# h is transposed one unit later in the last seven units of a gated cross-attention and mixture-of-experts kernel

## The reference

```python
def layernorm(x): return (x - mean(x)) / sqrt(var(x) + 1e-5)
# stage 1: attention over ctx, rotary embedding on q and k, masked softmax
q, k, v = layernorm(x) @ Wq, ctx @ Wk, ctx @ Wv
attn = softmax(mask(rope(q) @ rope(k).T / sqrt(128)))
x = x + tanh(g_xattn) * ((attn @ v) @ Wo)
# stage 2: router and experts on h = layernorm(x)
h = layernorm(x)
ratio = mean|h[text rows]| / (mean|h[vision rows]| + 1e-8)
scores = softmax([h, ratio] @ gate_w + gate_b)
top_val, top_idx = top_k(scores, 2)          # normalised; experts chosen by row 0 of the batch
expert_e(h) = act_e(h @ w1[e] + b1[e]) @ w2[e] + b2[e]   # act: tanh, gelu, silu
x = x + tanh(g_ffn) * sum_i top_val[i] * expert_(top_idx[i])(h)
```

## Time and profile before

| | us |
|---|---|
| median of 3 runs | 736.51 |
| the runs | 736.07, 736.51, 739.14 |
| profiled execution | 737.81 |
| its span | 736.0 |
| PE busy in the span | 704.6 (96%) |
| VectorE, ScalarE, GpSimd busy | 558.4, 357.0, 402.6 |
| drain of 7 units, from the first Y projection | from 574.12 |

### The profile page before, as it was taken

The page is one execution under the profiler, slowest core; times in us unless marked ns, Lnnn a source line. Parts: engine busy times, 40 slices in busy tenths (PEclk is TensorE's granted clock), DMA queues, the critical chain, the costliest instruction groups (busy, mean ns, idle before and its releaser), DMA issues.

```text
span 736.0 us, 11337 instructions
## 1 busy us (share of the span) xinstructions
PE 704.6 (96%) x3478; PEld 587.7 (80%) x3478; DVE 558.4 (76%) x924; ACT 357.0 (49%) x955; POOL 402.6 (55%) x340
## 2 busy tenths in 40 slices
PE   5798899899999999999999999999999879999998
PEld 3686688688888888888888888888888766788886
DVE  4977778778878787878888887878787984378832
ACT  5522452455554545454545545454545574872130
POOL 5653524665766666666657566666666541383020
PEclk9999999999999999999999999999999999999999
DMA  8695465432133131212213112222222310240101
GB/s 285 223 288 204 171 216 185 129 101 64 52 87 87 58 87 57 82 61 72 71 36 109 58 56 86 86 57 87 58 77 67 104 69 29 58 115 14 58 1 58
DMA packets 66111, 71.10 MB, mean 97 GB/s; under 512 B 8592, under 2 KB 42384, under 8 KB 66064
## 3 DMA queue, kind: packets, MB, share of 16 engines
q1 hardware_dynamic: 65680, 69.51, 30.1%
q0 software_dynamic: 384, 1.05, 0.4%
HBM read 51.66 MB, written 18.87 MB: 96 GB/s over the span
## 4 chain that ended last, share of the span: by engine, by line
PE 82%; DVE 6%; issue 5%; ACT 3%; POOL 3%; DMA 1%; SPq 0%; POOLq 0%; ACTq 0%; DVEq 0%
PE q L263 34%; PE y L253 28%; PE o L590 5%; PE s L542 5%; PE pt L464 4%; PE s L544 2%; PE o L253 1%; PE pt L253 1%; ACT prob L840 1%; POOL roped L1033 1%; DVE rot L1141 1%; DVE rot L1142 1%; DVE rot L1140 1%; DMA wraw<-in_L_xattn_Wk 1%; POOL scores L1033 1%
## 5 line engine op out<-in xcount | busy, mean ns | idle before, releaser
L263 PE MATMUL q<-xT_hi,big 128*128 128x512 f32 x704 | 235.9, 400 | 0.4 <-issue 0.4
L253 PE MATMUL y<-big,split 128*128 128x512 f32 (+1 forms) x784 | 193.0, 392 | 2.9 <-DVE split L1113 2.9
L253 PEld LDWEIGHTS y<-big,split 128*128 128x128 f32 x784 | 147.9, 189 | 34.5 <-DVE split L1113 3.9
L263 PEld LDWEIGHTS q<-xT_hi,big 128*128 128x128 f32 x704 | 132.2, 188 | 27.3 <-issue 0.6
L263 PE MATMUL q<-xT_lo,big 128*128 128x512 f32 x352 | 136.9, 389 | 0.0
L1060 POOL TENSOR_TENSOR roped<-rot 128x512 f32<-128x512 f32 x59 | 76.4, 1295 | 104.1 <-DVE rot L1142 104.1
L840 ACT ACTIVATE prob<-scores,nmax 128x128 f32<-128x128 f32 x256 | 99.8, 391 | 22.2 <-DVE nmax L1245 22.2
L828 ACT ACTIVATE big<-roped 128x512 fp32r<-128x512 f32 x64 | 40.5, 633 | 142.3 <-POOL roped L1060 137.6
L1076 POOL TENSOR_TENSOR prob<-prob,prec 128x512 f32<-128x512 f32 x64 | 66.6, 1040 | 50.7 <-DVE prec L1259 50.7
L1064 POOL TENSOR_TENSOR big<-roped,big 128x512 fp32r<-128x512 f32 x64 | 82.8, 1294 | 13.4 <-ACT big L828 13.4
L1052 POOL TENSOR_TENSOR big<-wraw,big 128x512 fp32r<-128x512 f32 x64 | 83.2, 1300 | 1.9 <-ACT big L820 1.9
(11 more groups left out here) (170 smaller groups left out, 1141.9 us busy)
## 6 DMA issues: line engine op xcount, KB each, us to landing
k_scratch<-split SPq DMA_DIRECT2D x16, 512.0 KB, 3.5
v_scratch<-split SPq DMA_DIRECT2D x16, 512.0 KB, 3.6
wraw<-in_L_xattn_Wq SPq DMA_DIRECT2D x32, 256.0 KB
wraw<-in_L_xattn_Wo SPq DMA_DIRECT2D x32, 256.0 KB
kv<-k_scratch SPq DMA_DIRECT2D x64, 128.0 KB, 2.5
kv<-v_scratch SPq DMA_DIRECT2D x64, 128.0 KB, 2.8
wraw<-in_L_ffn_w SPq DMA_DIRECT2D x28, 256.0 KB
rows<-ctx_t SPq DMA_DIRECT2D x8, 256.0 KB
```

The source lines that it names most:

```text
L253: mm = pe.matmul(bank_[:, :], stationary(s, c), moving(m, c), start=(c == 0 and n == 0), stop=(c == EC - 1 and n == 2))
L263: mm = pe.matmul(bank_[:, :].rearrange("p (b t) -> p b t", b=BH), weights[s][:, c, h * P:(h + 1) * P], source[m][:, half * BH:(half + 1) * ...
```

## The change

In the drain, PE transposes h of batch b - 2 instead of b - 1 in unit b, so that two more transposes lie behind it; `first_layer(0)` and `gate_products(0)` follow the Y projection of b = 6, and `first_layer(1)` the drain. ScalarE does the expert chunk after the exponentials, and the row and the h copy (now of batch b - 3) ahead of them. VectorE does `h_neg_mean` ahead of the scores, the h split (b - 3) ahead of the reciprocal, and `h_stats` at the end of the unit. GpSimd splits the expert chunk one unit later and does `h_pow` after the probabilities. No instruction is added or taken away.

```diff
--- before.py
+++ after.py
@@ -565,8 +565,7 @@
                 if past in VALUES_IN:
                     value_tile(2 * B - len(VALUES_IN) + VALUES_IN.index(past))
                 if drain and b == LAG_Y - 1:
-                    gate_products(0)
-                    first_layer(1)
+                    h_transpose(b - 2)
                 if not drain and past == LAG_Y:
                     pe.wait_ge(u_lo, 4 * B - 1)
                 if has(LAG_Y):
@@ -590,10 +589,11 @@
                         mm = pe.matmul(obank[:, :], kv[:, bs % NKV, 2 + s, :], split[:, 1, m, :],
                                        start=(n == 0), stop=(n == 2))
                     mm.then_inc(o_done, 1)
-                if drain and b >= 1:
-                    h_transpose(b - 1)
-                if drain and b == LAG_Y - 2:
+                if drain and 2 <= b < LAG_Y - 1:
+                    h_transpose(b - 2)
+                if drain and b == LAG_Y - 1:
                     first_layer(0)
+                    gate_products(0)
 
             def h_transpose(hb):
                 pe.wait_ge(h_row, hb + 1)
@@ -679,6 +679,8 @@
                 pe.matmul(sbank[:, 128:128 + B * NX], sel[:, 2, :], score.rearrange("p b e -> p (b e)"),
                           start=True, stop=True).then_inc(tok0_mm, 1)
 
+            h_transpose(B - 3)
+            first_layer(1)
             h_transpose(B - 2)
             first_layer(2)
             h_transpose(B - 1)
@@ -818,8 +820,6 @@
                     buf = wb[par] if b < EC else wa[1 - par]
                     act.wait_ge(w_in[b % NW], (g * 2 + ((W_A + b) // NW + 1)) * 16)
                     act.activation(buf[0][:, b % EC, :], wraw[:, b % NW, :], ACT.Copy).then_inc(w_hi, 1)
-                else:
-                    w_expert_hi(W_A + KVH * W_PER + b)
                 if has(1):
                     _, bq = lagged(par, b, 1)
                     act.wait_ge(q_roped, i)
@@ -831,6 +831,10 @@
                     if past >= LAG_P + 1:
                         act.wait_ge(o_done, i - LAG_P)
                     act.activation(split[:, 1, 0, :], pbank[:, :], ACT.Copy).then_inc(p_hi, 1)
+                if drain and b >= 1:
+                    norm_row(1, b - 1)
+                if drain and b >= 3:
+                    h_hi_(b - 3)
                 if has(LAG_S):
                     act.wait_ge(s_max, i - LAG_S + 1)
                     if past >= LAG_S + 1:
@@ -841,16 +845,13 @@
                                            bias=nmax[:, turn, h:h + 1], accum_out=psums[:, turn, h:h + 1])
                     a.then_inc(s_exp, 1)
                 if drain:
-                    if b >= 1:
-                        norm_row(1, b - 1)
+                    w_expert_hi(W_A + KVH * W_PER + b)
                     if b >= 2:
-                        h_hi_(b - 2)
                         sum_abs(b - 2)
                     if b == LAG_Y - 1:
                         norm_row(1, b)
-                        h_hi_(b - 1)
-                    if b >= LAG_S:
-                        first_act(b - LAG_S)
+                        h_hi_(b - 2)
+                        first_act(0)
 
             def s_done_before(t, bq):
 
@@ -934,9 +935,11 @@
 
 
             n = W_A + KVH * W_PER + LAG_Y
+            h_hi_(B - 3)
+            norm_row(1, B - 1)
             h_hi_(B - 2)
-            norm_row(1, B - 1)
             w_expert_hi(n)
+            first_act(1)
             gate_copy(0)
             first_act(2)
             h_hi_(B - 1)
@@ -1065,9 +1068,8 @@
                                        q_split(0, bq // BH, bq % HG).bitcast(F32), ALU.subtract).then_inc(q_lo, 1)
                 if past <= FILL:
                     weight_lo()
-                if drain:
-                    w_expert_lo(W_A + KVH * W_PER + b)
-                    h_pow(b)
+                if drain and b >= 1:
+                    w_expert_lo(W_A + KVH * W_PER + b - 1)
                 if has(LAG_S):
                     turn = (b - LAG_S) % 2
                     pool.wait_ge(s_rec, i - LAG_S + 1)
@@ -1077,8 +1079,7 @@
                                        prec[:, turn, :].unsqueeze(2).to_broadcast([P, HG, P]), ALU.mult
                                        ).then_inc(p_norm, 1)
                 if drain:
-                    if b == LAG_Y - 1:
-                        h_pow(B - 1)
+                    h_pow(b)
 
             def h_pow(hb):
 
@@ -1096,6 +1097,8 @@
             groups(pool, unit)
 
             n = W_A + KVH * W_PER + LAG_Y
+            w_expert_lo(n - 1)
+            h_pow(B - 1)
             for j in range(9):
                 w_expert_lo(n + j)
             for f in range(EC):
@@ -1232,6 +1235,8 @@
                     subtract_hi(split[:, 2, 1, :], obank[:, :], split[:, 2, 0, :], o_lo)
                 if past in VALUES_AT:
                     tile_lo(TILES_A + VALUES_AT.index(past))
+                if drain and b >= 1:
+                    h_neg_mean(b - 1)
                 if has(LAG_S):
                     turn, bs = (b - LAG_S) % 2, (b - LAG_S) % B
                     dve.wait_ge(s_done, i - LAG_S + 1)
@@ -1247,12 +1252,8 @@
                 if has(LAG_P):
                     dve.wait_ge(p_hi, i - LAG_P + 1)
                     subtract_hi(split[:, 1, 1, :], pbank[:, :], split[:, 1, 0, :], p_lo)
-                if drain:
-                    if b >= 1:
-                        h_neg_mean(b - 1)
-                    h_stats(b)
-                    if b == LAG_Y - 1:
-                        h_neg_mean(b)
+                if drain and b >= 3:
+                    h_lo_(b - 3)
                 if has(LAG_S):
                     turn = (b - LAG_S) % 2
                     dve.wait_ge(s_exp, i - LAG_S + 1)
@@ -1262,8 +1263,11 @@
                     dve.wait_ge(y_done, i - LAG_Y + 1)
                     dve.scalar_tensor_tensor(out=xacc[:, b3, :], in0=ybank[b3 % 2][:, :], scalar=gates[:, 0:1],
                                              in1=xacc[:, b3, :], op0=ALU.mult, op1=ALU.add).then_inc(y_acc, 1)
-                if drain and b >= 2:
-                    h_lo_(b - 2)
+                if drain:
+                    h_stats(b)
+                    if b == LAG_Y - 1:
+                        h_neg_mean(b)
+
             def h_lo_(hb):
                 dve.wait_ge(h_hi, hb + 1)
                 subtract_hi(xT[1][:, hb, :, :].rearrange("p c t -> p (c t)"), h_bank(hb)[:, :],
@@ -1285,6 +1289,7 @@
                                          in1=rstd[:, 1, hb:hb + 1], op0=ALU.mult, op1=ALU.mult).then_inc(h_nmr, 1)
 
             groups(dve, unit)
+            h_lo_(B - 4)
             h_stats(B - 1)
             h_lo_(B - 3)
             h_neg_mean(B - 1)
```

## The result

The changed kernel takes 742.2 us in the median (741.52 to 744.35, 4 runs) beside 736.8 for the kernel before (now also 4 runs): ratio 1.0076, 95% interval 1.0048 to 1.0105. It is slower by about 5.4 us, where I had forecast 736.2 and no difference that could be told. Its profiled execution took 741.53, its span is 739.7 (736.0 before).

The account below looks back on a forecast made before the run. TensorE's reaching its fifth first-layer tile was taken to bound the kernel. Terms 0.29 - 1.61 - 0.58 - 1.32 + 0.38 + 1.13 = -1.71 gave 736.1 from the profiled 737.81, -0.10 without clock gave 736.4 from the median; forecast 736.2, range 734.9 to 738.0.

Parts of the forecast that it names:

- What bounds the kernel: TensorE's reaching first_layer(4), 631.82 before, decides; anything taken from or added ahead of it moves the end by the same amount.
- The period: Drain units, first exponential to next: 6.41 us against 6.74, including a 0.13 stall and 0.07 slot for the mean.
- The edits costed at nothing: Moved expert chunks, GpSimd's later split and power, and first_act: no cost, with bounds together of -0.3 to +1.3 us.
- From the exponentials of unit 4 to Y of unit 5: End of the drain's ring: exponentials at 601.78, O split 605.21, Y projection 605.94 where it was 605.65, so +0.29 us.
- The clock, -1.61: Unit 5's Y projection: its clock dip, 4.60 against 2.99 us, does not come back; rival that it stays: 737.7, chance 0.17.
- The wait before the first tile, -0.58: TensorE before the first expert tile: 0.96 shrinks to a transpose's slot of 0.38, as Y of unit 6 stands between.
- The wait before the last transposes, -1.32: TensorE before 623.57: the wait is gone, since a 12-matmul tile now separates each two of the last transposes.
- one transpose more, +0.38: TensorE after unit 5's Y projection: the transpose of h of batch 3 now lies behind it, adding 0.38 us.
- the wait before Y of unit 6, +1.13: TensorE is ready at 610.22, but the O split queued on VectorE lets Y start only at 611.35: +1.13 us.
- The sum without clock, -0.10: All path terms up to first_layer(4) without the clock term total -0.10 us: the waits change places.
- Rival 2: Slower: VectorE's new wait for the power heads each unit; period stays 6.74, price 1.3 us, 737.4 or 739.0; chance 0.13.
- Range and chances: Whole kernel: 734.9 to 738.0 us; chance 0.03 faster by over 0.5%, 0.03 slower, 0.94 within.

Follow-up runs that it names:

- e1: Changed kernel plus one wait: in the drain GpSimd splits the expert chunk only after VectorE's mean; 737.12 us, ratio 0.9998 to the kernel before.
- e4: Changed kernel with one-tensor-input mean, h_stats ahead of the reciprocal, O copy straight after the exponentials, GpSimd's old order; 732.12 us, ratio 0.9941 to the kernel before.
- after_again: The changed kernel run again unaltered; 741.83 us, ratio 1.0080 to the kernel before.
- e2: Changed kernel with the mean as tensor_scalar, one tensor input and a pointer scalar, instead of two tensor inputs; 737.02 us, ratio 1.0001 to the kernel before.
- e3: Changed kernel with GpSimd's split of the drain's expert chunks issued as two instructions of 256 columns; 737.81 us, ratio 1.0024 to the kernel before.
- after: The changed kernel itself, first measurement and profile, against the kernel before; 742.2 us in the median, ratio 1.0076.
- e5: Kernel before the change with only the mean put in the form with one tensor input; 736.5 us, ratio 1.0003 to the kernel before.
- e6: The short-ring version e4 with the mean back in the form with two tensor inputs; 735.22 us, ratio 0.9978 to the kernel before.

## Why the prediction was wrong

Point by point, by its own steps:

- **What bounds the kernel.** Held for the two kernels: the time of `first_layer(4)` decides, 104.2 us follow it in both. That whatever is saved ahead of it "moves the end by the same amount" is too strong: in `e1` to `e4` 1.6 us come back behind it by the clock.
- **The period.** This is the step that failed: "a new stall of 0.13, and 0.07 for its own slot", with a mean of 0.16 read from a row in which GpSimd was idle. With the mean at 1.24 the slot is 1.16 (601.91 to 603.07) and 6.41 becomes 7.50; measured 7.49. Everything else in the period was right to a hundredth: with the hold removed the period is 6.41, and the four periods take 25.66 us where I had 25.64. Forecast for four: 25.64; measured after the change: 29.97. Of the 6.3 us by which the stretch to `first_layer(4)` came out longer than forecast (60.27 against 55.68 - 1.71 = 53.97), that is 4.3; 1.2 lie between Y of unit 5 and Y of unit 6 (mostly the dip) and 0.8 behind it.
- **The edits costed at nothing.** The other half of the same mistake: "On GpSimd the split of a chunk comes one unit later, ahead of the probability multiply, where the engine would wait for the reciprocal anyway". True for GpSimd; but I asked only what the moved instruction delays on its own engine and who waits for its result, and not what it runs beside. It begins when the power ends, which is also what releases the mean.
- **From the exponentials of unit 4 to Y of unit 5.** Forecast 605.94 - 601.78 = 4.16; measured 609.39 - 605.23 = 4.16. The handover of 0.04 in it is a slight misreading: from O split to Y the rows have 598.92 - 598.17 = 0.75, not 0.73.
- **The clock, -1.61.** Not given back in the profiled execution, given back in the others: none of `after_again`, `e1`, `e2` and `e3` has a dip in that projection. `after` and `after_again` are one kernel, with about the same stretch of transposes and waiting ahead of the projection (2.1 us), and one has the dip and the other not. It comes and goes between executions, so it should not have been a term of a sum that is compared with a median. I gave that rival 0.17; it was true of one of two profiles of the changed kernel, and the loss is there in both.
- **The wait before the first tile, -0.58.** Gone in the forecast; after the change 619.42 - 616.01 = 3.41 remains where 2.83 is Y's slot, so 0.58 of waiting, since the row of batch 5 stands behind a held mean, and the h copy and its split behind that row. In the run with the added wait it is gone.
- **The wait before the last transposes, -1.32, one transpose more, +0.38, the wait before Y of unit 6, +1.13.** As forecast: from Y of unit 5 to Y of unit 6 I had 5.41, the run with the added wait has 5.47, and no profile of the new order waits before the last transposes.
- **The sum without clock, -0.10.** Kernel before at full clock 54.16 (`e5`), change without the hold 54.14 (`e1`): -0.02, and ratios of 0.9998 and 1.0001. So the new order in itself is worth nothing, as forecast, and the hold is worth 59.26 - 54.14 = 5.1 us: 4.3 in four periods, 0.15 from Y of unit 5 to Y of unit 6, 0.7 behind it. The medians agree: 5.4 us lost with the hold (5.1 in `after_again`), 0.2 without.
- **Rival 2** put the danger at the right place, VectorE's new wait at the head of each unit, but with the wrong mechanism (late handovers) and so with a price of 1.3 instead of 5.1. I argued against it that "all three are taken from rows". They were; the row of the third was one without GpSimd beside it.
- **Range and chances.** The 0.03 for slower by over 0.5% followed from having bounded the mean from above by nothing. The trace of before gave the bound: 1.26.

The Trainium skill, "SBUF — State Buffer", section "Who interferes with whom", states the rule: a VectorE instruction with two SBUF inputs contends with a GpSimd instruction that reads SBUF, and whichever comes second is fully blocked, as the port pair that they share is an exclusive lock; one with at most one SBUF input, outside the two-port performance modes, does not contend. The runs agree, for the case that GpSimd came first, the only one they show: 1.24 against 0.21 us for the two forms, and the end of the mean with the end of GpSimd's instruction within 0.03 us in `e3` and `e6`. Had I applied that rule to my own sum, the slot of the mean would have been the split's 1.29 us, and the forecast some 5 us higher, an estimate (4 x (1.29 - 0.07) = 4.9).

## What to carry to other kernels

When an instruction is moved, ask what it will run beside on other engines, not only what it delays on its own; two instructions released by the same event meet again in every unit, as here, and a [128, 1] instruction can then cost as much as the other's whole tile. Take a duration from rows in the new neighbourhood, and look for the longest of the same instruction in the trace before calling it small: the group's mean (302 ns for an instruction of 150) was the sign here. Two remedies gave the whole loss back here: a form that takes the per-partition factor as a scalar pointer instead of a second tensor, and a wait that lets the tiny instruction go first.

## What the runs showed of the hardware

- A `scalar_tensor_tensor` on [128, 1] with both tensors in SBUF lasted from 0.15 to 1.26 us: 0.15 or 0.16 alone, otherwise up to the end of GpSimd's instruction in flight, to within 0.03 us, be that a split or a probability multiply. Both of these read SBUF; a GpSimd instruction that only writes was not tried. With the split cut in halves, the mean got in between them (0.69). The same product as `tensor_scalar` with a pointer took 0.20 to 0.21 beside GpSimd and alone.
- VectorE's instructions with one tensor in PSUM and one in SBUF kept their time beside GpSimd: the scores' first addition 0.68 us, the Y accumulation 0.72.
- Two executions of the changed kernel differ by a dip of TensorE's clock in the drain (0.69 over one projection) at a price of 1.0 us; the kernel before, with the dip, and `e5`, without, by 1.5.
- The clock also fell with PE busy throughout: behind 16 matmuls of 8x4, in four of nine profiles (0.94 over 612 to 640 in `e1`), at a price of 1.6 us.
